# A bias product inside an MLP loop: a diagonal matrix and two fp32 products per tile, or one transposed row triple and two one-pass products

## The reference, cut to what matters

```
dqx = round(x * s) / s            with s = 127 / max|x| of the row
dqw = clip(round(w * sw), -1, 1) / sw
h = dqx @ dqw.T + b1              # 256 -> 1024
h = gelu(h); h = layernorm(h) * g2 + c2
h = (the same with w2, b2)        # 1024 -> 256
```

## Time and profile before

| | us |
|---|---|
| median of 3 runs (lowest, highest) | 1132.0 (1130.74, 1132.81) |
| the profiled execution's own time | 1130.56 |
| its span, from the first to the last instruction | 1128.8 |
| its mean granted TensorE clock | 0.959 of full speed |
| the MLP phase in it | from about 915 to the end |

### The profile page before, as it was taken

One profiled execution on the slowest core, in us unless ns is written; L12 is line 12 of the kernel. 1 busy time (PEld: TensorE's weight loads), 2 busy tenths in 40 slices (PEclk: granted clock), 3 DMA queues, 4 the chain that ended last, 5 costly groups with the idle time before them and its releaser, 6 DMA issues. The chain is left out here.

```text
span 1128.8 us, 24959 instructions
## 1 busy us (share of the span) xinstructions
PE 993.1 (88%) x9226; PEld 783.2 (69%) x9226; DVE 825.2 (73%) x1997; ACT 583.2 (52%) x1094; POOL 492.1 (44%) x493
## 2 busy tenths in 40 slices
PE   5898989994799999999999967999999957888886
PEld 4676777773588888888888855777777724445444
DVE  4688887775757667667666574777777738988896
ACT  2465666654433333333332245666666527777875
POOL 2344444443123223223232313444444438999990
PEclk9799999997799999999999977999999979999997
DMA  7600000000000000000000030000000000000000
GB/s 223 184 2 2 2 2 2 2 3 1 1 1 1 0 0 0 0 0 0 0 0 0 1 144 2 2 3 1 3 2 2 2 1 10 24 24 19 25 24 29
DMA packets 19421, 20.98 MB, mean 19 GB/s; under 512 B 6528, under 2 KB 17920, under 8 KB 19072
## 3 DMA queue, kind: packets, MB, share of 16 engines
q1 hardware_dynamic: 17712, 19.12, 5.4%
q10 hardware_dynamic: 1616, 0.58, 0.3%
HBM read 15.51 MB, written 4.19 MB: 17 GB/s over the span
## 5 line engine op out<-in xcount | busy, mean ns | idle before, releaser
L435 POOL TENSOR_TENSOR sm_a<-sm_a,mx_a 128x616 f32<-128x616 f32 x128 | 155.7, 1217 | 257.2 <-DVE mx_a L607 257.2
L746 POOL TENSOR_TENSOR hl_f<-hf_f,hh_f 128x512 fp32r<-128x512 f32 x80 | 103.5, 1294 | 261.4 <-ACT hh_f L870 261.4
L865 ACT ACTIVATE sg_f<-pGU_f 128x512 f32<-128x512 f32 x80 | 47.9, 599 | 169.1 <-PE pGU_f L771 169.0
L600 DVE TENSOR_TENSOR sm_a<-pS_a,mask 128x616 f32<-128x616 f32 x128 | 101.1, 792 | 38.4 <-PE pS_a L477 38.4
L769 PE MATMUL pGU_f<-xh_f,wgh_f 128*128 (+1 forms) x320 | 128.4, 401 | 0.0
L770 PE MATMUL pGU_f<-xl_f,wgh_f 128*128 (+1 forms) x320 | 124.9, 390 | 0.0
L771 PE MATMUL pGU_f<-xh_f,wgl_f 128*128 (+1 forms) x320 | 124.9, 390 | 0.0
L976 DVE TENSOR_TENSOR hf_f<-pGU_f,sg_f 128x512 f32<-128x512 f32 x80 | 55.3, 691 | 91.7 <-ACT sg_f L865 91.7
L986 DVE SCALAR_TENSOR_TENSOR x<-pD_f,coef_f,x 128x256 f32 (+1 forms) x256 | 106.2, 477 | 17.3 <-PE pD_f L808 15.9
L557 ACT ACTIVATE pr_a<-sm_a 128x616 f32<-128x616 f32 x128 | 91.5, 715 | 49.1 <-POOL sm_a L435 49.1
L506 PE MATMUL pO_a<-pt_a,V 128*32 128x128 f32 x2048 | 104.4, 276 | 2.1 <-DVE x L632 2.1
(11 more groups left out here) (196 smaller groups left out, 2257.4 us busy)
## 6 DMA issues: line engine op xcount, KB each, us to landing
x<-x_in SPq DMA_DIRECT2D x4, 1024.0 KB, 10.7
out_x<-x SPq DMA_DIRECT2D x32, 128.0 KB, 1.7
gu<-gu_in SPq DMA_DIRECT2D x1, 2560.0 KB, 9.4
aw<-aw_in SPq DMA_DIRECT2D x2, 1024.0 KB, 10.5
w<-w_in SPq DMA_DIRECT2D x2, 1024.0 KB, 6.2
dn<-dn_in SPq DMA_DIRECT2D x1, 1280.0 KB, 12.0
b<-b_in SPq DMA_DIRECT2D x1, 512.0 KB, 8.9
g<-g_in SPq DMA_DIRECT2D x1, 512.0 KB, 9.7
```

The lines of the kernel that those rows point to most:

```text
L435: pool.tensor_tensor(heads, heads, mx[u][:, g, :].rearrange("p (h a) -> p h a", a=1).broadcast_to([P, HG, SK]), ALU.subtract).then_inc(shi ...
L600: dve.tensor_tensor(sm[u][:, g, :].rearrange("p (b h k) -> p b h k", b=2, k=SK), pS[:, 2 * g:2 * g + 2, 0:HS].rearrange("p b (h k) -> p b ...
L746: pool.tensor_tensor(hl[u][:], hf[u][:], f32(hh[u][:]), ALU.subtract).then_inc(hl_ok, 1)
```

## The change

Instead of a diagonal, three rows are multiplied. inv is split into a part `hi` that a one-pass float32r operand holds exactly and the rest `lo`, b1 likewise into `bh` and `bl`; then inv * b1 is taken as hi*bh + hi*bl + lo*bh, a product over three rows of a [3, 128] operand (hi, hi, lo) and a [3, 1024] operand (bh, bl, bh).

- GpSimd: `terms` takes the place of `diagonal`: a cast of inv to two float32r columns of `iv` and, after a wait for that cast, the subtraction that gives the third. Its buffer wait is now for `qat_ps` and not for `up_ps`.
- TensorE: `turn_x` gets a third transpose, of `iv` (128x3 to 3x128), ahead of which it waits for `terms`; `offset` is two one-pass products over three rows, waits for ScalarE's copies, and stands behind `turn_h`.
- ScalarE: `x_turned` gets a second copy, of the transposed three rows from PSUM to SBUF (`ivt`), and signals after it.
- GpSimd in the attention of layer 1: `offset_rows` makes the [3, 1024] operand `b3` from b1 once, in four pieces after the steps t = 8, 10, 12 and 14, seven instructions in all (two of them over one pass of 1024 with a factor per partition in the third piece).

```diff
+TERMS = 3
...
+            def offset_rows(n):
+                b1, b3, low = sb["b1"][0:TERMS, :], sb["b3"][:], sb["b1_low"][:]
+                second, others = sb["ident"][0:TERMS, 1:2], sb["others"][:]
+                if n == 0:
+                    pool.wait_ge(sb["mlp_in"], 16 * len(MLP_ROWS))
+                    pool.tensor_scalar(others, second, -1.0, 1.0, ALU.mult, ALU.add)
+                    pool.tensor_copy(b3, b1).then_inc(sb["b3_step"], 1)
+                if n == 1:
+                    pool.wait_ge(sb["b3_step"], 1)
+                    pool.tensor_tensor(low, b1, b3.bitcast(F32), ALU.subtract).then_inc(sb["b3_step"], 1)
+                if n == 2:
+                    pool.wait_ge(sb["b3_step"], 2)
+                    pool.tensor_scalar(low, low, second, 1.0, ALU.mult, ALU.mult).then_inc(sb["b3_step"], 1)
+                    pool.tensor_scalar(b3, b3.bitcast(F32), others, 1.0, ALU.mult, ALU.mult).then_inc(sb["b3_step"], 1)
+                if n == 3:
+                    pool.wait_ge(sb["b3_step"], 4)
+                    pool.tensor_tensor(b3, b3.bitcast(F32), low, ALU.add).then_inc(sb["b3_step"], 1)
+
+            def full(t, u, has):
+                step(t, u, has)
+                if layer == 1 and 8 <= t < 16 and t % 2 == 0:
+                    offset_rows((t - 8) // 2)
...
-        dg = [sbt(f"dg{i}", [P, P]) for i in range(2)]
+        iv = [sbt(f"iv{i}", [P, TERMS], F32R) for i in range(2)]
+        ivt = [sbt(f"ivt{i}", [TERMS, P], F32R) for i in range(2)]
...
-            def diagonal(t, u):
+            def terms(t, u):
                 pool.wait_ge(xs_ok, 3 * t + 3)
                 if t >= 2:
-                    pool.wait_ge(up_ps, t - 1)
-                pool.tensor_scalar(dg[u][:], sb["ident"][:], col(sa[u], 4), 1.0, ALU.mult, ALU.mult).then_inc(diag_ok, 1)
+                    pool.wait_ge(qat_ps, t - 1)
+                pool.tensor_copy(iv[u][:, 0:TERMS - 1], col(sa[u], 4).broadcast_to([P, TERMS - 1])).then_inc(diag_ok, 1)
+                pool.wait_ge(diag_ok, 2 * t + 1)
+                pool.tensor_tensor(iv[u][:, TERMS - 1:TERMS], col(sa[u], 4), iv[u][:, 0:1].bitcast(F32),
+                                   ALU.subtract).then_inc(diag_ok, 1)
...
-                    mm = pe.transpose(pA[:, k * P:(k + 1) * P], ha[u][:, k * P:(k + 1) * P], sb["ident"][:])
-                mm.then_inc(qat_ps, 1)
+                    pe.transpose(pA[:, k * P:(k + 1) * P], ha[u][:, k * P:(k + 1) * P], sb["ident"][:])
+                pe.wait_ge(diag_ok, 2 * t + 2)
+                pe.transpose(pA[0:TERMS, G * P:(G + 1) * P], iv[u][:].bitcast(F32), sb["ident"][:]).then_inc(qat_ps, 1)
 
             def offset(t, u):
-                pe.wait_ge(diag_ok, t + 1)
+                pe.wait_ge(qat_sb, t + 1)
...
-                    pe.matmul(pU[u][:, half_row], dg[u][:], sb["b1"][:, half_row], start=True, stop=False)
+                    pe.matmul(pU[u][:, half_row], ivt[u][:], sb["b3"][:, half_row], start=True, stop=False)
...
                 if has(4):
                     turn_x(t + 4, u)
-                    offset(t + 4, u)
                 if has(1):
                     turn_h(t + 1, 1 - u)
                 if has(4):
+                    offset(t + 4, u)
                     up(t + 4, u)
...
-                act.activation(qat[u][:].rearrange("p k n -> p (k n)"), pA[:, 0:D], ACT.Copy,
-                               bias=-MAGIC).then_inc(qat_sb, 1)
+                act.activation(qat[u][:].rearrange("p k n -> p (k n)"), pA[:, 0:D], ACT.Copy, bias=-MAGIC)
+                act.activation(ivt[u][:], pA[0:TERMS, G * P:(G + 1) * P], ACT.Copy).then_inc(qat_sb, 1)
```

More of the change, by code:

```diff
@@ L447, in step @@
                     bias(t + 1)
-            lay_out_steps(step, 3, 1)
+            def offset_rows(n):
[19 more added lines that the diff above has]
+                    offset_rows((t - 8) // 2)
+            lay_out_steps(full, 3, 1)
         @block.tensor
@@ L1132, in step @@
                 if has(5):
-                    diagonal(t + 5, 1 - u)
+                    terms(t + 5, 1 - u)
                 if has(3):
@@ L1400, in build @@
             keep(name, [P, w])
+        keep("b3", [TERMS, HID], F32R)
+        keep("b1_low", [TERMS, HID])
+        keep("others", [TERMS, 1])
+        sb["b3_step"] = ctx.enter_context(nc.semaphore("b3_step"))
         keep("q1", [P, G, HID], BF16)
```

## The result

The change makes the kernel slower: the median of four runs is **1159.2 us** (1155.89 to 1164.45) against 1131.37 for the kernel before, a ratio of 1.025 with a 95% interval of 1.021 to 1.030. The forecast was 1135.1 in a range of 1129.6 to 1141. The direction was right and the size wrong by a factor of nine (27.8 us slower for 3.1 forecast); of the cases, it was the clock, which had 8%.

What follows compares the result with a forecast made beforehand. The prediction took VectorE's own work plus the 0.55 us root as the bound. Its terms, 3.9 - 1.2 + 0.4 = +3.1 us on 1130.56, gave 1133.7, and a median of 1135.1 us, range 1129.6 to 1141.

Steps and rivals of the forecast that it cites:

- the clock: Rival case: TensorE, less busy, falls to 1.2 GHz and the kernel is slower by much, 1145 us or more; chance 0.08.
- What bounds the kernel: MLP step of 5.93 us: VectorE's own work plus 0.55 us of root; removing the diagonal wins some 0.01 us a step.
- TensorE gets 1.1 to 1.4 us freer a step, which is worth 0: MLP, TensorE: cheaper offset products free time, but existing waiting covers it, so no gain.
- rival 2: MLP: TensorE's clock falls because it is less busy, 1145 us or more; chance 0.08.
- The loop above 9: MLP at 1.2 GHz: the loop over TensorE and ScalarE would take 9 us.
- every second step lost 1 us: +13: MLP: assumed loss if the clock falls, +13 us in all, giving 1145 us or more.
- my 5.5 us: MLP at full clock: the summed loop over TensorE and ScalarE, 5.5 us against 6.08 for the new step.
- The cast kept off by `centre`, +3.9 us: MLP, GpSimd: cast waits out `centre`, subtraction follows, root 0.15 us later in 26 steps: +3.9 us (3.1 to 7.5).
- rival 1: MLP, GpSimd: cast gets ahead of `centre`, only the subtraction waits, root 0.07 us later a step: 1133.0 us; chance 0.20.
- The steps that are like this one: MLP: the 26 steps where the diagonal started first yet lost to `centre`, held against the cast getting ahead.
- The start, -1.2 us: Start of the MLP: cheaper offset products at half clock shorten the first gelu's wait, -1.2 us (0 to -2.4).
- Attention, +0.4: Attention of layer 1: the added instructions for b3 delay one step's shift, +0.4 us (0 to 2.9).

Runs made afterwards that it cites:

- old_order_fill2: The change with its offset products ahead of the transposes of h and two dummy fp32 products of 128x256 on TensorE: 1131.84 us, 1.003.
- fill3: The change with three dummy fp32 products of 128x256 a step on TensorE between the transposes of x and h: 1133.68 us, 1.002.
- fill1: The change with one dummy fp32 product of 128x256 a step on TensorE ahead of the transposes of h: 1135.19 us, 1.004.
- order_only: The kernel before, with only its two offset products moved behind the transposes of h: 1143.06 us, 1.011.
- old_order: The change, with its two one-pass offset products moved back ahead of the transposes of h: 1131.34 us, 1.002.
- one_pass_diag: The kernel before, with diagonal and b1 as float32r, so the offset is two one-pass products over 128 rows: 1129.01 us, 0.999.
- rows_only: The kernel before, with `offset_rows` added in the attention of layer 1 and its result unused: 1130.09 us, 1.000.
- rows128: The change, with iv, ivt and b3 on 128 rows, 125 rows of ivt being zero: 1137.75 us, 1.007.
- gap_before: The kernel before, with VectorE's result and largest |x| moved ahead of `scale`: 1129.1 us, 0.999.

## Why the prediction was wrong

**What bounds the kernel: right.** The diagonal and the variance end a tie, and taking the diagonal away wins nothing. Steps at full clock are 5.93 before and 5.94 after, and old_order_fill2 shows the same by a run. The kernel before shows it too: the diagonal at 944.70 took 0.40 us (rows below), and its step was still 5.93.

**"TensorE gets 1.1 to 1.4 us freer a step, which is worth 0": this step failed.** It is true at 2.4 GHz (and the time is nearer 1.0: 1.98 went, and 0.73 and 0.27 came). But the freed time itself lowers the clock: three dummy products hold it at 0.99, and without them it is 0.82. I had weighed that as rival 2, from one window at 60% in which 2.4 GHz held, and one such window was too little for a chance of 8%. fill3 shows it. The Trainium skill, in "TensorE: Matmul & The Clock Gate", section "Part 1: The HAM clock gate (the "warmup" mystery)", says that the clock is set by how busy TensorE has been recently. The trace agrees in that more work raised it (0.82 to 0.99), and fill1 beside order_only shows that the busy share is not all of it.

**"The loop above 9" and "every second step lost 1 us: +13": the ring was named, its price was wrong.** At full clock my 5.5 us stood up: the ring that follows the slow step is 5.58. At half clock it is 8.45 us, 2.5 above the 5.94 of VectorE's loop, not 1. I had written 9 and then priced the rival at 1 us a step in thirteen steps; 27.4 us over 31 steps are 0.88 each. I also took 5.5 against 6.08 as "fits, with little to spare" and let it go there. **The comparison that was missing is the ring at 1.2 GHz against 5.94.**

**The order was priced at nothing.** I followed the wait for `diag_ok` to ScalarE's copies and the lateness it brings (1.2 us), but did not say that TensorE had used ScalarE's rounding to do the offset, and that behind `turn_h` the offset is a link of the ring. order_only (+12.5 us at a clock of 1.00) and old_order (+1.7 us at 0.92) show that this decides. It takes both: low clock with the old order costs 0 to 2 us (one_pass_diag, old_order), the new order with the clock held (fill3) 2 to 3, both together 28. The clock isn't the same in these, 0.92 in the old order and 0.82 in the new one; that the order itself moves the clock is part of what it costs.

**The cast kept off by `centre`, +3.9 us: wrong, and rival 1 was right.** The cast starts 0.10 us ahead of `centre` and takes 0.23; it is the subtraction that waits (1.12). The rule that the prediction cited from the Trainium skill, "SBUF — State Buffer", section "SBUF: two separate sides", fits the cast's 0.23 us, though not the diagonal's 1.50, as far as recorded starts can tell who was first. It isn't the width that decides: the kernel before had steps in which the diagonal won too. There it starts 0.09 ahead of `centre` and not 0.06:

```profile
944.70 0.40 POOL L1123 TENSOR_SCALAR dg_m<-ident,sa_m 128x128 f32<-128x128 f32 x1
...
944.79 1.39 DVE L1260 SCALAR_TENSOR_TENSOR hn_m<-ge_m,se_m,g 128x1024 f32<-128x1024 f32 x1
```

In all 26 steps in which the diagonal took 1.50 it led by 0.06 or 0.07 us, in the four in which it took 0.39 to 0.41 by 0.09 to 0.13, and the cast of the change leads by 0.10 or more. "The steps that are like this one", which the prediction held against rival 1, are those with the short lead. Rival 1's +0.07 a step was too high as well: the root comes no later, and the step grows by 0.01 or less.

**The start, -1.2 us: the term was right, its worth was not.** The first gelu comes 13.43 us after the MLP's start (ScalarE's table load, 914.37 and 915.24) instead of 14.59, which is 1.16:

```profile
924.73 1.21 PE L1184 MATMUL pU_m<-b,ivt_m 3*128 3x512 f32 x2 [0.62 <-ACT ivt_m L1233]
...
927.80 1.11 ACT L1257 ACTIVATE ge_m<-pU_m,sa_m 128x1024 f32<-128x1024 f32 x1 [1.82 <-PE pU_m L1191]
```

But the first `scale` is only 0.3 earlier, and at the low clock the next steps lose more (7.68 and 7.54). Even fill3 has an 8.32 there.

**Attention, +0.4: nothing** (rows_only). The burst was half as long as estimated.

Not settled is why the low stretches are so much longer in the change than in one_pass_diag or old_order, and this makes up much of the loss. A longer ring leaves TensorE more often waiting, which would keep the clock low and the ring long; the runs fit that, but none tests it by itself.

## What to carry to other kernels

Before you take work off TensorE, add up the ring of products, copies and handoffs through it twice, at 2.4 and at 1.2 GHz, and compare both with the step; if only the first fits, the "free" time can cost more than the work did. That is a warning and not yet a price: at 1.2 GHz the rings of the change (8.45) and of old_order (7.64) are both above 5.94, and they cost 28 and 2 us; in the second the low stretches stayed shorter than a step. A product that runs while its engine would wait for another one anyway is worth its place: moved behind that wait, it is a link of the ring. When two parts of a change are suspected, run each alone and both together, since here neither alone came near the 28 us. And when you fill a gap on VectorE, look at what GpSimd does at the moment to which the work is shifted.

## What the runs showed of the hardware

- A GpSimd cast of 128x2 that starts 0.10 us ahead of VectorE's pass over 1024 columns is done in 0.23 us; a pass over 128 columns in the same place took 1.50 where it was 0.06 or 0.07 ahead (26 steps) and 0.40 where it was 0.09 ahead. Which of the two engines goes first turned between 0.07 and 0.09 us of recorded lead in the kernel before.
- From the first of two products over three rows to the product over 128 rows behind them it is 0.67 us, where the two are over 128 rows 0.54 (fill3, rows128).
- The granted clock over 159 us was 1.00 with TensorE busy for 118.95 us (order_only), and 0.93 with 123.22 (fill1). How the work lies matters, not only how much of it there is; what in it matters isn't settled.
- VectorE and GpSimd hold each other off in one-input passes too: `round_x` over 256 columns took 0.80 us beside an addition on GpSimd (gap_before), and 0.33 without.
- The ring with a short low stretch in it (clock 0.73 to 0.76) is 6.22 us in one_pass_diag, 6.50 in old_order and 7.19 in the change; at full clock all three fit into 5.94.
